# Opening the y accumulation with transposed skip terms made on GpSimd, in place of fp32 products with a diagonal matrix

## The chip, the cores and the metric

The kernel runs on one core of one Trainium2 chip. The metric is the device time of one execution in microseconds (us), the median of several runs. Engines are named PE (TensorE; PEld is its weight load), DVE (VectorE), ACT (ScalarE), POOL (GpSimd) and SP (SyncE, which issues the DMAs here).

## The reference, cut to what matters

Two batches of 1024 tokens with 128 features go through a block with two Mamba scans (forward and backward in time) and then a mixture of experts. What the change touches is the skip term `xc * Dsk`, one scalar of `Dsk` per inner channel (256 channels):

```python
xc = silu(conv(xh))                                   # [B, L, DI], DI = 256
delta = softplus(dt @ dt_w.T + dt_b)
h = h * exp(d_t[:, :, None] * A) + (d_t * u_t)[:, :, None] * B_t[:, None, :]   # 16 states
y = einsum('bds,bs->bd', h, C_t) over all t, + xc * Dsk
y = y * silu(z)
return y @ out_proj.T
```

## The kernel before, in words

The work is cut into four units `u` (two batches by two directions). Within a unit there are 16 states by two halves of 128 channels, so 32 steps; the whole kernel has 128 steps `e`, and step `t` of a unit is `e % 32`. A half has its 128 channels on the partitions and the 1024 tokens along the free dimension.

One step passes through four engines:

- ACT makes the decay `dA` (L565, 128x1024) and scales blocks of `duT` by `B` into `dBuT` (L572, eight 128x256 instructions for each state).
- PE turns (transposes, L1202) the blocks of `dBuT` into PSUM tiles `dBu`, two chunks of 512 tokens. There are three such tiles in turn, so a chunk waits for the scan of the chunk three before it (`scan_done`).
- DVE runs the scan on both chunks (L980 forward, L984 backward) into `hs`, of which there are three buffers. Scan `e` therefore waits until the product `e-3` is done (`hc_done`).
- POOL multiplies `hs` by the row `C` into `hc` (L481, 128x1024). It waits for both scan chunks of the step, for the row's DMA and, from three steps on, for PE to have added the `hc` of three steps before.
- PE adds `hc` to the PSUM accumulator `yT` by eight turns, `y_add(e)` (L1202). PE issues it two steps later, behind the `dBu` chunks of step `e+3` of its order and behind the projection work of that step.

PE's order of a step is written out by hand: both chunks of `dBu(e+1)`, then the step's part of the next unit's projections (items `X`, `Z`, `B`, `BT`, `DT`, `DU`, or the last unit's `YT` and `O`), then `y_start` where `t` is 2 or 3, then `y_add(e-2)`. `turn` at L1202 and `mm` at L1198 are helpers, so nearly all PE instructions have one of these two lines.

`y_start(u, half)` opens the accumulator of a half: it waits until DVE has gated the unit before (`gate_done`, L993), and then multiplies each of eight 128x128 blocks of `xc` with a diagonal matrix `dskip` that holds `D`. An fp32 product is two weight loads and two matmuls in the trace, so one `y_start` is 16 of each.

POOL's order: initial fills, two powers `rstd`, then the loop over all steps. At `t` = 23 and 24 of the first three units it makes `du` of the next unit (L459, 128x1024, two inputs) ahead of that step's product. `du` needs `delta` of the next unit, which ACT makes in two softplus instructions at `t` = 22 (L555) out of the buffer `pre`. The buffer `pre` is then idle until ACT writes it again in the next unit (items `DT`, L540, behind the items `B` and `BT`).

At the start DVE finishes `xc` of unit 0 in two halves (L782, semaphore `x0_ready`) and goes on to scale weights (L823, L825, L830), keep gate rows (L802) and make tap weights (L818).

Of the kernel before, what the change touches and what calls it, by code (L numbers as in the profile page):

```python
# [7 lines left out]
DI, DS, DC, DR = 256, 16, 4, 64  # L8
E, TOPK, F = 8, 64, 512
P = 128  # L10
NH = DI // P
NBLK = L // P
CH = 512
NCH = L // CH
BPC = CH // P
XD = DR + 2 * DS
NU = 2 * NB
# [13 lines left out]
WAT, WCOLS = {}, 0  # L31
# [75 lines left out]
def count_of(it, kinds):  # L107

    return sum(o[0] in kinds for o in ORDER[:NUMBER[it] + 1])


def product_at(e):

    u, t = divmod(e, DS * NH)
    if u + 1 == NU or t not in (SP_AT + 1, SP_AT + 2):
        return None
    return t - SP_AT - 1


def build_block(nc, x_d, mod_d, wpack_d, bcast_d, dtw_d, w1_d, w2_d, crow_d, out_d):  # L120
    fp32 = mybir.dt.float32
    ALU = mybir.AluOpType
# [3 lines left out]
    with ctx:  # L126
        def sb(name, shape):
            return ctx.enter_context(nc.sbuf_tensor(name, shape, fp32))

        def pb(name, shape):  # L130
            return ctx.enter_context(nc.psum_tensor(name, shape, fp32))

        def sem(name):
            return ctx.enter_context(nc.semaphore(name))
# [5 lines left out]
        wp = sb("wp", [P, WCOLS])  # L140
# [8 lines left out]
        xc = [area1[:, p, 0] for p in range(2)]  # L149
# [5 lines left out]
        pre = sb("pre", [P, NH, L])  # L155
# [7 lines left out]
        Cb = area3[:, 3:6, :]  # L163
        yg = area3[:, 6:6 + NH, :]
        du = yg
        wtap = sb("wtap", [P, 2, DC, DI])
        Aneg = sb("Aneg", [P, 2, NH, DS])
        dskip = sb("dskip", [P, 2, NH, P])
# [16 lines left out]
        yT = pb("yT", [P, NH, NBLK, P])  # L185
# [24 lines left out]
        s_w = sem("weights_loaded")  # L210
# [21 lines left out]
        x0_ready = sem("first_x_ready")  # L232
# [9 lines left out]
        tanh_ready = sem("tanh_ready")  # L242
        delta_ready = sem("delta_ready")
        du_ready = sem("du_ready")
        c_stored = sem("c_stored")
        cb_ready = [sem(f"cb_ready{i}") for i in range(3)]
        da_ready = sem("da_ready")
# [54 lines left out]
        def unit(u):  # L302
            return u // 2, u % 2, u % 2

        def wait_item(eng, *it):

            if it[0] in BY_ACT:
                eng.wait_ge(item_act, count_of(it, BY_ACT))
            else:
                eng.wait_ge(item_dve, count_of(it, BY_DVE))  # L310
# [5 lines left out]
        def wait_delta(eng, half, u):  # L316

            if u == 0:
                wait_item(eng, "DT", half * NCH + NCH - 1, 0)
            else:  # L320
                eng.wait_ge(delta_ready, NH * (u - 1) + half + 1)
# [105 lines left out]
        @block.gpsimd  # L427
        def _(g_):
            g_.memset(ident[:, :], 0.0).then_inc(s_c, 1)
            g_.memset(ones[:, :], 1.0).then_inc(s_c, 1)  # L430
            g_.memset(mhalf[:, :], -0.5).then_inc(s_c, 1)
            g_.memset(ones3[:, :], 1.0).then_inc(s_c, 1)
            g_.memset(hT[:, :, :], 0.0).then_inc(s_c, 1)
            g_.memset(emask[:, :, :], 0.0).then_inc(s_c, 1)
            g_.iota(iotak[:, :], [[1, TOPK]], base=1, channel_multiplier=0,
                    allow_small_or_imprecise_dtypes=True).then_inc(s_c, 1)
            g_.wait_ge(s_c, 7)
            g_.affine_select(out=ident[:, :], in_=ident[:, :], compare_op=ALU.not_equal, fill=1.0, base=0,
                             pattern=[[-1, P]], channel_multiplier=1).then_inc(s_c, 1)
            g_.wait_ge(s_c, 8)  # L440

            g_.affine_select(out=emask[0:64, :, :], in_=emask[0:64, :, :], compare_op=ALU.not_equal, fill=1.0,
                             base=0, pattern=[[-2, NPAIR], [1, E]], channel_multiplier=0).then_inc(s_c, 1)
            g_.wait_ge(s_c, 9)
            g_.affine_select(out=emask[64:P, :, :], in_=emask[64:P, :, :], compare_op=ALU.not_equal, fill=1.0,
                             base=-1, pattern=[[-2, NPAIR], [1, E]], channel_multiplier=0).then_inc(s_c, 1)
            g_.wait_ge(s_c, 10)

            for b in range(NB):
                rs = slice(b * NBLK, (b + 1) * NBLK)  # L450
                g_.wait_ge(xvar_ready, b + 1)
                g_.tensor_tensor(rstd[:, rs], rstd[:, rs], mhalf[:, rs], ALU.pow).then_inc(xrstd_ready, 1)

            def pool_du(half, u):
                _, _, par = unit(u)
                wait_delta(g_, half, u)
                for c in range(NCH):
                    wait_item(g_, "X", half * NCH + c, u)
                g_.tensor_tensor(du[:, half, :], delta[par][:, half, :], xc[par][:, half, :],  # L459
                                 ALU.mult).then_inc(du_ready, 1)  # L460

            pows = [0]

            def rstd_pow(b):

                pows[0] += 1
                g_.wait_ge(var_ready, pows[0])
                rs = slice(b * NBLK, (b + 1) * NBLK)
                g_.tensor_tensor(rstd[:, rs], rstd[:, rs], mhalf[:, rs], ALU.pow).then_inc(rstd_ready, 1)

            for e in range(NT):
                g = e // NH
                if product_at(e) is not None:
                    pool_du(product_at(e), e // (DS * NH) + 1)
                if e == NT - 1:
                    break
                g_.wait_ge(scan_done, NCH * (e + 1))
                g_.wait_ge(cb_ready[g % 3], 16 * (g // 3 + 1))
                if e >= 3:
                    g_.wait_ge(yacc_done, e - 2)  # L480
                g_.tensor_tensor(hc[:, e % 3, :], hs[:, e % 3, :], Cb[:, g % 3, :], ALU.mult).then_inc(hc_done, 1)  # L481
                if e - NH * DS * (NU - 2) in POW_AT:
                    rstd_pow(0)
                if e == 0:

                    g_.memset(ones16[:, :], 1.0).then_inc(upto_ready, 1)
                    g_.wait_ge(upto_ready, 1)
                    g_.affine_select(out=upto[:, :], in_=ones16[:, :], compare_op=ALU.is_ge, fill=0.0, base=0,
                                     pattern=[[1, P]], channel_multiplier=-1).then_inc(upto_ready, 1)

            for n in range(2):
                rstd_pow(1)

        @block.scalar
        def _(act):
# [55 lines left out]
            def softplus(u):  # L551
                _, _, par = unit(u)
                wait_item(act, "DT", NH * NCH - 1, u)
                for half in range(NH):
                    nc.scalar.activation(delta[par][:, half, :], pre[:, half, :], ACT.Softplus).then_inc(delta_ready, 1)  # L555

            def exp_tile(e):

                u, s, half = e // (DS * NH), e // NH % DS, e % NH
                _, dr, par = unit(u)  # L560
                if s == 0:
                    wait_delta(act, half, u)
                if e >= 3:
                    act.wait_ge(scan_done, NCH * (e - 2))
                nc.scalar.activation(dA[:, e % 3, :], delta[par][:, half, :], ACT.Exp,  # L565
                                     scale=Aneg[:, dr, half, s:s + 1]).then_inc(da_ready, 1)

            def scale_block(g, n):

                u, s = divmod(g, DS)  # L570
                _, _, par = unit(u)
                return nc.scalar.activation(dBuT[:, g % 2, n, :], duT[par][:, n, :], ACT.Copy,  # L572
                                            scale=bT[:, par, n, s:s + 1])
# [622 lines left out]
        def _(pe):  # L1196
            def mm(out, lhsT, rhs, start, stop):
                return nc.tensor.matmul(out, lhsT, rhs, start=start, stop=stop, skip_group_check=True)  # L1198

            def turn(out, in_, start, idn=None):  # L1200

                return nc.tensor.matmul(out, in_, ident[:, :] if idn is None else idn, start=start, stop=True,  # L1202
                                        is_transpose=True, skip_group_check=True)
# [155 lines left out]
            def y_start(u, half):  # L1359

                _, dr, par = unit(u)
                if u > 0:
                    pe.wait_ge(gate_done, NH * (u - 1) + half + 1)
                for n in range(NBLK):
                    mm(yT[:, half, n, :], xc[par][:, half, n * P:(n + 1) * P], dskip[:, dr, half, :],
                       n % BPC == 0, True)

# [28 lines left out]
            for e in range(NT):  # L1396
                u, t = divmod(e, DS * NH)
# [185 lines left out]
```

## Time and profile before

| | us |
|---|---|
| median of 3 runs | 596.76 (596.41 to 598.2) |
| the profiled execution | 597.98 |
| its span, first to last instruction | 596.2 |
| mean granted TensorE clock | 0.946 |
| PE, DVE, ACT, POOL busy | 497.6, 466.6, 445.2, 330.5 |

A busy time is the sum of an engine's instructions. A row of the timeline gives the start, the duration, engine, line, operation, tiles, shapes and count; the bracket at its end is the idle time of that engine just before, and what ended it. Rows that follow each other on one engine overlap a little, so the time that a group really occupies is read from start to start, or from the chain of waits, which follows the instruction that ended last back to what released it.

### The profile page before, as it was taken

To read this page: it belongs to the slowest core of one execution; us is meant where nothing else is said; L and a number is where in the kernel's file an instruction comes from. 1 tells how busy PE (TensorE), PEld (TensorE's weight loads), DVE (VectorE), ACT (ScalarE), POOL (GpSimd) and SP (SyncE) were. 2 spreads that over 40 slices of the span, in tenths; PEclk is the share of its full clock that TensorE was granted. 3 is DMA by queue.
4 is the path that set the end of the run, shared out by engine and by line. 5 is a ranking of instruction groups with operands and counts; after the bars stand their busy time and mean duration, and the time that the engine had idled before them with its cause. 6 is when DMAs were issued, how large, how long until landed. Compare 5 with 4: busy or idle time off the path is not lost.

```text
span 596.2 us, 9244 instructions
## 1 busy us (share of the span) xinstructions
PE 497.6 (83%) x3378; PEld 409.0 (69%) x3378; DVE 466.6 (78%) x709; ACT 445.2 (75%) x847; POOL 330.5 (55%) x155
## 2 busy tenths in 40 slices
PE   3578979996899999698998896778967486999997
PEld 2245856876788678586965676678856375788696
DVE  5866887976978777699799985988999999866422
ACT  2459865999998789999975899987979761274250
POOL 3104645867966677696766777957667673200000
PEclk9888998998999999799999997979989989978999
DMA  7031120321322222123220231312272214000101
GB/s 256 0 110 37 71 71 36 101 75 38 111 85 90 74 72 71 59 87 106 73 72 35 72 107 36 111 47 95 71 212 76 86 53 142 0 1 2 35 1 36
DMA packets 17885, 43.46 MB, mean 73 GB/s; under 512 B 1328, under 2 KB 7600, under 8 KB 17584
## 3 DMA queue, kind: packets, MB, share of 16 engines
q1 hardware_dynamic: 17840, 42.87, 21.9%
q8 instruction: 27, 0.44, 0.3%
q14 instruction: 18, 0.15, 0.1%
HBM read 41.56 MB, written 1.31 MB: 72 GB/s over the span
## 4 chain that ended last, share of the span: by engine, by line
PE 40%; ACT 28%; DVE 23%; issue 6%; POOL 1%; DMA 1%; POOLq 0%; DVEq 0%; ACTq 0%
ACT dBuT L572 13%; PE pro L1198 11%; DVE area L984 9%; PE yT L1198 9%; PE yT L1202 8%; ACT dA L565 8%; PE dBu L1202 6%; PE dBu L1198 4%; DVE area L980 3%; PE pro L1202 2%; DVE area L772 1%; ACT pre L540 1%; ACT th L533 1%; DVE pre L954 1%; ACT area L555 1%
## 5 line engine op out<-in xcount | busy, mean ns | idle before, releaser
L481 POOL TENSOR_TENSOR hc<-area 128x1024 f32<-128x1024 f32 x127 | 303.2, 2390 | 159.6 <-DVE area L980 92.4
L572 ACT ACTIVATE dBuT<-area,bT 128x256 f32<-128x256 f32 x508 | 215.1, 498 | 13.8 <-PE dBu L1202 13.7
L1202 PE MATMUL dBu<-ident,dBuT 128*128 128x128 f32 x1024 | 147.2, 281 | 43.3 <-DVE area L984 23.5
L565 ACT ACTIVATE dA<-area,Aneg 128x1024 f32<-128x1024 f32 x128 | 146.1, 1142 | 20.3 <-DVE area L984 13.5
L1202 PEld LDWEIGHTS dBu<-ident,dBuT 128*128 128x128 f32 x1024 | 118.1, 144 | 57.3 <-issue 21.3
L1202 PE MATMUL yT<-ident,hc 128*128 128x128 f32 x1024 | 140.3, 282 | 1.7 <-POOL hc L481 1.4
L1202 PEld LDWEIGHTS yT<-ident,hc 128*128 128x128 f32 x1024 | 120.7, 145 | 20.6 <-issue 16.4
L984 DVE TENSOR_TENSOR_SCAN area<-dA,area,dBu 128x512 f32<-128x512 f32 x64 | 81.8, 1278 | 4.5
L980 DVE TENSOR_TENSOR_SCAN area<-dA,area,dBu 128x512 f32<-128x512 f32 x64 | 81.8, 1278 | 4.1
L980 DVE TENSOR_TENSOR_SCAN area<-dA,dBu 128x512 f32<-128x512 f32 x64 | 77.1, 1205 | 7.7 <-PE dBu L1202 7.0
L984 DVE TENSOR_TENSOR_SCAN area<-dA,dBu 128x512 f32<-128x512 f32 x64 | 77.1, 1205 | 6.5 <-PE dBu L1202 6.0
L1198 PE MATMUL pro<-hT,wtap 128*128 128x512 f32 x96 | 48.0, 624 | 0.2 <-DVE area L869 0.2
L1198 PE MATMUL pro<-wp,hT 128*128 128x256 f32 (+1 forms) x96 | 23.2, 372 | 14.3 <-DVE area L869 12.6
L869 DVE SCALAR_TENSOR_TENSOR area<-th,pro 128x512 f32<-128x512 f32 x16 | 11.0, 688 | 25.8 <-ACT th L533 25.3
L533 ACT ACTIVATE th<-pro 128x512 f32<-128x512 f32 x28 | 16.5, 588 | 19.3 <-PE pro L1198 19.3
L1198 PEld LDWEIGHTS pro<-wp,hT 128*128 128x128 f32 x96 | 15.6, 201 | 18.2 <-DVE area L869 14.6
L1202 PE MATMUL pro<-ident,area 128*128 128x128 f32 x108 | 17.4, 285 | 11.2 <-DVE area L869 4.8
L1198 PEld LDWEIGHTS pro<-hT,wtap 128*128 128x128 f32 x96 | 17.3, 201 | 13.3 <-issue 12.6
L1202 PEld LDWEIGHTS pro<-ident,area 128*128 128x128 f32 x108 | 12.2, 143 | 14.2 <-DVE area L869 5.5
L641 ACT ACTIVATE hc<-dBu,modT 128x512 f32<-128x512 f32 x2 | 1.6, 780 | 25.7 <-PE dBu L1198 25.7
L670 ACT ACTIVATE hc<-yT,wp 128x64 f32<-128x64 f32 x64 | 14.0, 330 | 8.5 <-PE yT L1198 8.4
L1198 PE MATMUL pro<-area,wp 128*96 128x512 f32 x28 | 14.7, 643 | 6.3 <-DVE area L782 6.3
(227 smaller groups left out, 570.1 us busy)
## 6 DMA issues: line engine op xcount, KB each, us to landing
area<-c_rows SPq DMA_DIRECT2D x64, 512.0 KB, 3.7
dBuT<-w_in SPq DMA_DIRECT2D x1, 2048.0 KB, 9.2
wp<-wpack_in SPq DMA_DIRECT2D x1, 1030.0 KB, 7.5
x<-x_in SPq DMA_DIRECT2D x2, 512.0 KB, 6.5
hc<-bcast_in SPq DMA_DIRECT2D x1, 1024.0 KB, 10.5
out<-x SPq DMA_DIRECT2D x4, 256.0 KB, 2.4
hT<-w_in SPq DMA_DIRECT2D x1, 512.0 KB, 7.3
acc<-w_in SPq DMA_DIRECT2D x1, 512.0 KB, 7.5
```

The costliest lines, as they stand in the source:

```text
L481: g_.tensor_tensor(hc[:, e % 3, :], hs[:, e % 3, :], Cb[:, g % 3, :], ALU.mult).then_inc(hc_done, 1)
L533: nc.scalar.activation(th[:, :], src, ACT.Tanh).then_inc(tanh_ready, 1)
L540: nc.scalar.activation(dst[:, half, c * CH:(c + 1) * CH], src, func, bias=dtb(dr, half)).then_inc(item_act, 1)
L555: nc.scalar.activation(delta[par][:, half, :], pre[:, half, :], ACT.Softplus).then_inc(delta_ready, 1)
L565: nc.scalar.activation(dA[:, e % 3, :], delta[par][:, half, :], ACT.Exp, scale=Aneg[:, dr, half, s:s + 1]).then_inc(da_ready, 1)
L572: return nc.scalar.activation(dBuT[:, g % 2, n, :], duT[par][:, n, :], ACT.Copy, scale=bT[:, par, n, s:s + 1])
L670: last = nc.scalar.activation(hid[:, q % 2, i, c, :], up_bank(q)[:, at:at + TOPK], ACT.Gelu_apprx_tanh, bias=b1c[:, 2 * q + i, c:c + 1])
L869: nc.vector.scalar_tensor_tensor(gz[par][:, 2 * j:2 * j + 2, :].rearrange("p n d -> p (n d)"), th[:, :], 1.0, src, ALU.add, ALU.mult).then ...
L980: nc.vector.tensor_tensor_scan(hs[:, e % 3, lo:hi], dA[:, e % 3, lo:hi], dBu[q % 3][:, :], init, ALU.mult, ALU.add).then_inc(scan_done, 1)
L984: nc.vector.tensor_tensor_scan(hs[:, e % 3, lo:hi][:, ::-1], dA[:, e % 3, lo:hi][:, ::-1], dBu[q % 3][:, ::-1], init, ALU.mult, ALU.add).t ...
L1198: return nc.tensor.matmul(out, lhsT, rhs, start=start, stop=stop, skip_group_check=True)
L1202: return nc.tensor.matmul(out, in_, ident[:, :] if idn is None else idn, start=start, stop=True, is_transpose=True, skip_group_check=True)
```

## The change: what it does

POOL gets a new instruction, `skip_term(half, u)`: one multiplication of `xc` (128x1024, fp32) by a column of `D`, written to `skip`, which is the buffer `pre` under another name. It is made for units 0, 1 and 2. For unit 0 both halves stand ahead of POOL's loop and wait for `x0_ready`. For units 1 and 2 they stand at `t` = 25 and 26 of the unit before, ahead of that step's product, and wait for `delta_ready` (so that the softplus has read `pre`). In `y_start` of those units PE waits for `skip_ready` and then issues eight turns of `skip` in place of eight fp32 products. The last unit keeps the products, and the diagonal matrices are still built.

```diff
+        skip = pre
+        skip_ready = sem("skip_term_ready")
+            def skip_term(half, u):
+                _, dr, par = unit(u)
+                at = WAT["dskip"] + dr * NH + half
+                if u == 0:
+                    g_.wait_ge(s_w, 16)
+                    g_.wait_ge(x0_ready, half + 1)
+                else:
+                    for c in range(NCH):
+                        wait_item(g_, "X", half * NCH + c, u)
+                    g_.wait_ge(delta_ready, NH * (u - 1) + half + 1)
+                g_.tensor_scalar(skip[:, half, :], xc[par][:, half, :], wp[:, at:at + 1], None,
+                                 ALU.mult).then_inc(skip_ready, 1)
...
+            for half in range(NH):
+                skip_term(half, 0)
             for e in range(NT):
                 g = e // NH
                 if product_at(e) is not None:
                     pool_du(product_at(e), e // (DS * NH) + 1)
+                if product_at(e - 2) is not None and e // (DS * NH) < NU - 2:
+                    skip_term(product_at(e - 2), e // (DS * NH) + 1)
...
             def y_start(u, half):
                 if u > 0:
                     pe.wait_ge(gate_done, NH * (u - 1) + half + 1)
+                if u + 1 < NU:
+                    pe.wait_ge(skip_ready, NH * u + half + 1)
                 for n in range(NBLK):
+                    if u + 1 < NU:
+                        turn(yT[:, half, n, :], skip[:, half, n * P:(n + 1) * P], n % BPC == 0)
+                        continue
                     mm(yT[:, half, n, :], xc[par][:, half, n * P:(n + 1) * P], dskip[:, dr, half, :],
                        n % BPC == 0, True)
```

## Rows read from the trace of the kernel before

**Rows 1.** The chain that ended last, its shares of the span by engine.

```profile
PE 40%; ACT 28%; DVE 23%; issue 6%; POOL 1%; DMA 1%; POOLq 0%; DVEq 0%; ACTq 0%
```

**Rows 2.** The groups of PE's instructions that touch yT: busy us, mean ns, idle before.

```profile
L1202 PE MATMUL yT<-ident,hc 128*128 128x128 f32 x1024 | 140.3, 282 | 1.7 <-POOL hc L481 1.4 <-DVE hc L1118 0.3
L1198 PE MATMUL yT<-dskip,area 128*128 128x128 f32 x128 | 15.7, 276 | 0.0
```

**Rows 3.** The chain of waits, unit 0's opening: start us, us, what.

```profile
57.50 1.78 PE yT L1198 x16
59.28 0.87 PE yT L1202 x8
...
61.89 1.78 PE yT L1198 x16
```

**Rows 4.** Timeline of ACT behind unit 0's opening.

```profile
61.93 0.60 ACT L533 ACTIVATE th<-pro 128x512 f32<-128x512 f32 x1 [0.58 <-PE pro L1198]
...
65.03 1.71 ACT L572 ACTIVATE dBuT<-area,bT 128x256 f32<-128x256 f32 x4 [1.46 <-PE dBu L1202]
```

**Rows 5.** The chain of waits from the end of unit 0 to unit 1's opening.

```profile
160.11 0.66 PE dBu L1202 x4
...
171.61 1.79 PE yT L1198 x16
```

**Rows 6.** Timeline of ACT behind the openings of units 1 and 2.

```profile
178.71 1.71 ACT L572 ACTIVATE dBuT<-area,bT 128x256 f32<-128x256 f32 x4 [1.40 <-PE dBu L1202]
...
289.12 1.31 ACT L572 ACTIVATE dBuT<-area,bT 128x256 f32<-128x256 f32 x3 [1.46 <-PE dBu L1202]
```

**Rows 7.** The groups of POOL's instructions: busy us, mean ns, idle before.

```profile
L481 POOL TENSOR_TENSOR hc<-area 128x1024 f32<-128x1024 f32 x127 | 303.2, 2390 | 159.6 <-DVE area L980 92.4 <-DVE area L984 53.6 <-PE yT L1202 8.8
L433 POOL MEMSET hT<- 128x2060 f32 x1 | 1.8, 1804 | 0.0
L438 POOL TENSOR_SCALAR_AFFINE_SELECT ident<-ident 128x128 f32<-128x128 f32 x1 | 0.3, 292 | 0.2 <-POOL iotak L435 0.2
L445 POOL TENSOR_SCALAR_AFFINE_SELECT emask<-emask 64x32 f32<-64x32 f32 x1 | 0.2, 226 | 0.1
L429 POOL MEMSET ident<- 128x128 f32 x1 | 0.2, 204 | 0.3 <-POOLq L1576 0.3
```

**Rows 8.** The end of unit 0 as one stretch: us, busy of PE, PEld, DVE, ACT, POOL, PEclk, DMA share, GB/s.

```profile
142.00:160.00 18.00, 15.11 (x128) 13.77 (x126) 17.15 (x15) 17.73 (x35) 18.00 (x9) 0.99 0.28 94
```

**Rows 9.** Timelines at unit 0's end: POOL product 26, DVE scans 29 and 32, PE.

```profile
149.54 2.39 POOL L481 TENSOR_TENSOR hc<-area 128x1024 f32<-128x1024 f32 x1
...
152.78 1.19 DVE L980 TENSOR_TENSOR_SCAN area<-dA,dBu 128x512 f32<-128x512 f32 x1
160.27 1.20 DVE L984 TENSOR_TENSOR_SCAN area<-dA,dBu 128x512 f32<-128x512 f32 x1
...
161.47 1.04 PE L1202 MATMUL dBu<-ident,dBuT 128*128 128x128 f32 x8
164.07 0.60 PE L1202 MATMUL yT<-ident,hc 128*128 128x128 f32 x4
```

**Rows 10.** Timelines at unit 1's end: POOL products 57 and 58, DVE scan 61.

```profile
256.21 2.37 POOL L481 TENSOR_TENSOR hc<-area 128x1024 f32<-128x1024 f32 x1 [0.43 <-DVE area L984]
258.70 2.37 POOL L481 TENSOR_TENSOR hc<-area 128x1024 f32<-128x1024 f32 x1
...
263.53 1.20 DVE L984 TENSOR_TENSOR_SCAN area<-dA,dBu 128x512 f32<-128x512 f32 x1
```

**Rows 11.** One group of DVE's L954: count, ns min/median/max, first and last start.

```profile
L954 DVE TENSOR_SCALAR acc<-acc,mv,rstd x8: 323/334/2370, 314.0 to 317.8; 128x128 f32<-128x128 f32 x8
```

**Rows 12.** Timeline of DVE at the start, behind its weight work.

```profile
36.10 0.29 DVE L877 COPY bT<-yT 128x128 f32<-128x128 f32 x1 [1.87 <-PE yT L1202]
38.75 1.23 DVE L787 TENSOR_TENSOR area<-area 128x1024 f32<-128x1024 f32 x1 [2.35 <-ACT area L540]
```

**Rows 13.** The chain of waits behind PE's idle stretch before 139 us.

```profile
140.14 1.71 PE yT L1202 x8
```

## The prediction

> **What bounds the kernel now.** I read the chain of waits first, then the timelines of the engines around the places that the change touches, then the groups. The chain lies on PE for 40% of the span, on ACT for 28 and on DVE for 23 [rows 1], so no busy share decides: each place has to be looked at by itself. Where the accumulators open, the chain runs through PE. In unit 0 the two openings stand on it with 1.78 us each [rows 3], in unit 1 with 1.79 us [rows 5], whose second, at 175.58 us, and the two of unit 2, at 282 and 286 us, repeat the row. Behind each pair ACT sits idle until a dBu tile comes from PE: 0.58 and 1.46 us in unit 0 [rows 4], 1.40 and 1.46 us in units 1 and 2 [rows 6]. These idle times are the most that a faster PE can hand on there. At the end of unit 0 it is different: POOL is busy for 18.00 of 18.00 us, ACT for 17.73 and DVE for 17.15 [rows 8]. POOL's two new instructions of unit 1 fall into just this stretch.
>
> **What PE saves.** An fp32 product is two passes in the trace: 64 products are 128 matmuls [rows 2]. Their own durations (276 against 282 ns) say nothing, since they overlap; the chain gives what a group occupies. Sixteen passes take 1.78 to 1.79 us and eight turns 0.87 us [rows 3, 5]. An opening made of turns thus saves 1.79 - 0.87 = 0.92 us, and a pair 1.84 us. Six openings change, 5.5 us of PE work in all. Unit 3's keep their products.
>
> **What of it counts.** Unit 0: the first opening moves the tanh of ACT earlier by 0.58 us, then ACT is its own limit; at the dBuT group ACT has that 0.58 plus 1.46 us, over 1.84, so all 1.84 us pass through. Unit 1: ACT is busy without a gap until 1.40 us before 178.71 us, so at most 1.40 us pass. Unit 2: at most 1.46 us. Without a cost elsewhere this is 1.84 + 1.40 + 1.46 = 4.70 us. From there on ACT, DVE, POOL and the C rows' DMAs all follow the same steps, and no load from outside is due, so I take the gain as kept.
>
> **What one multiplication costs on POOL.** The trace shows no such instruction at this size. From below: a fill takes (1804 - 204) / (2060 - 128) = 0.83 ns per column, so 1024 columns take 204 + 896 x 0.83 = 0.95 us; the affine selects, which read and write, give (292 - 226) / (128 - 32) = 0.69 ns per column and 0.91 us [rows 7]. From above: the same size with two inputs takes 2.36 to 2.39 us [rows 7]. The new instruction reads one tile and writes one, as the select does, so I take X = 1.0 us and keep 0.9 and 2.36.
>
> A page leaves room for more. The Trainium skill, GPSIMD Engine Reference, section "Performance versus the Vector engine", has 1.03 cycles per element at 1.2 GHz for the lightest loop bodies and about 1.8 for a tight loop with more in it, estimates of 0.88 and 1.54 us here; by the dearer one the sum below would be 3.3 us of gain instead of 4.4. The short rows of this trace stand near the first, but no run shows the size in question.
>
> **Where it delays, unit 0's end.** The first multiplication stands ahead of product 25, the second ahead of product 26, and POOL has no gap to take them. Product 26 ended at 149.54 + 2.39 = 151.93 us, scan 29, which waits for its buffer, began at 152.78 [rows 9]. The slack is 0.85 us, so with X = 1.0 scan 29 is 2.0 - 0.85 = 1.15 us late. Behind it DVE runs back to back and doesn't catch up. What waits for DVE is PE: the second chunk of dBu(33), at 161.47 + 4 x 0.11 = 161.91 us, needs the tile that the first chunk of scan 32 frees at 160.27 + 1.20 = 161.47 us; a slack of about 0.4. PE comes 1.15 - 0.4 = 0.75 us late, and it is on the chain from there to unit 1's openings [rows 5]. y_add(30), at 164.07 us, is not hit: product 30, four products further, ended at about 151.93 + 4 x 2.36 = 161.4, a slack of 2.7 us, more than 2X. Queued behind the two multiplications are POOL's products alone; it issues no DMA. PE's pair of openings then has 1.84 - 0.75 = 1.09 us to give, under the cap of 1.40. Unit 1's share falls from 1.40 to 1.09 us.
>
> **Unit 1's end.** Product 58 ended at 261.07 us, scan 61 began at 263.53: 2.46 us of slack, and POOL has a gap of 0.43 us ahead of product 57 [rows 10]. With PE's 0.4 us of slack behind DVE this covers 2X up to 3.3 us: no cost up to X = 1.6 us.
>
> **The start.** Unit 0's multiplications come as soon as the halves of `xc` are finished, around 29 to 31 us; POOL's loop has nothing to do until the first scan. DVE then has its TENSOR_SCALAR instructions (L823 to L830). One such instruction, 334 ns in the median, took 2370 ns once, beside a product of POOL [rows 11]; so they may be held for as long as POOL works, some 1 to 2 us. DVE then waits 1.87 us for PE and 2.35 us for ACT [rows 12], which covers it; without this cover the start would be 1 to 2 us longer. The B products need only `xc`, which is finished before. The new wait of PE for `skip_ready` is met some 20 us or more before each opening.
>
> **The sum.** 1.84 + 1.09 + 1.46 = 4.4 us. The profiled execution's own time is 597.98 us, its span of 596.2 and 1.8 around it; it would be 593.6. It is 1.2 us above the median of 596.76, from which the same gain gives 592.4 us, the forecast.
>
> **The rivals.** A first one is that the multiplication costs what a two-input product does, X = 2.36 us. Scan 29 is then 4.72 - 0.85 = 3.87 us late and PE 3.47, so unit 1's share is 1.84 - 3.47 = -1.63 us. At unit 1's end PE is 4.72 - 0.43 - 2.46 - 0.4 = 1.43 us late, so unit 2's share is 0.41. The sum is 0.6 us of gain, 596.1 us. For it speaks that POOL has no other full-size row; against it the slopes of rows 7.
>
> The second ends on the other side: the multiplication with a column operand runs far below the rate of the shorter rows, at twice a product's time, 4.7 us. Along the same steps the sum is 1.84 + (3.09 - 2X) + (5.13 - 2X) = 10.1 - 4X, so the change costs time from X = 2.5 us, and 4.7 us would cost 8.7 us, 605.5 us. For it speaks only that no row shows a column operand on POOL; every row of the group lies far below.
>
> The third is that the clock does not hold under turns. At the lower of its two levels eight turns take 1.71 us [rows 13]. Openings of turns would then save 0.08 us each, and the sum is 0.16 + (0.16 - 0.75) + 0.16 = -0.3, 597.0 us; each further group of eight turns at that level would add 0.84. Against it: in the stretch from 142 to 160 us PE did nothing but turns, and the granted clock was 0.99, so the full 2.4 GHz [rows 8]. The Trainium skill, TensorE: Matmul & The Clock Gate, section "PE-mode transpose", says that the full clock does not engage for transpose mode; by that rule the turns would be at 1.2 GHz, and the trace disagrees.
>
> The fourth is that only part arrives: the gain is used up later where other engines were equally late (DVE's gates, the first norm), leaving 1 to 2 us, 595.3 us. The chain's steady passing between PE and ACT speaks for it a little; that all engines shift together speaks against.
>
> **How the numbers follow.** I give my forecast 0.72, the two-input price 0.08, the dear multiplication 0.04, the clock 0.03 and the partial gain 0.13. The forecast's own range runs from X = 0.9 with no loss, 4.7 us, to 3 us of gain, and 1 us either way for the clock's steps: 591.0 to 594.8. The range takes in the two-input and the partial case, 591.0 to 596.2 us. A difference under 0.3% (1.8 us) can't be told from none here. Faster by more than that is the forecast and half of the partial case, 0.78; the rest of that case and the two-input price make 0.15 within it; slower 0.07.
>
> **What would show it.** Right, if the chain shows the openings of units 0 to 2 as eight turns of 0.87 us; if POOL's new group has six instructions of about 1.0 us; if scan 29 comes about 1.2 us later against scan 26 than now, and PE's idle time there grows; if ACT's idle time behind units 1 and 2's openings nearly vanishes. Wrong, if the new group's mean lies above 1.6 us, if PE or DVE wait for POOL at the end of unit 1 too, if the granted clock falls in the openings, or if unit 0's first opening, at 57.5 us, moves.

## The result: 599.71 us against 597.3 us, a little slower

The changed kernel has a median of 599.71 us in 14 runs, the kernel before 597.3 us in 14 runs beside it. The ratio of the changed kernel to the one before is 1.0036, with a 95% interval of 1.002 to 1.0052. The profiled execution took 599.41 us, its span is 597.7 us, the mean granted clock 0.94 (before: 0.946). In the experiments below, four executions fell in a slower state (600.29 and 728.93 us with the later multiplications, 950.73 us with turns only, 605.32 us with unit 0 alone): the medians count them, the ratios don't.

The chain of the changed kernel by engine, and who waits for POOL's products (us in total, times, longest):

```profile
PE 41%; DVE 25%; ACT 20%; issue 8%; POOL 3%; DMA 1%; POOLq 0%; DVEq 0%; ACTq 0%
```

```profile
PE yT L1222 <- POOL hc L501: 7.3, 6, 2.0
...
DVE area L1000 <- POOL hc L501: 4.7, 2, 2.5
DVE area L1004 <- POOL hc L501: 2.4, 1, 2.4
```

Against [rows 1] ACT has lost 8 points of the chain, and POOL and idle "issue" time have come in. DVE's waits for POOL's products are new, and PE's had been 1.4 us. The line numbers are 20 higher than before from L481 on.

**The price.** The new instruction on POOL: count, ns min/median/max, first and last start.

```profile
L475 POOL TENSOR_SCALAR pre<-area,wp x6: 2837/2883/4826, 29.0 to 261.6; 128x1024 f32<-128x1024 f32 x6
```

The forecast put 1.0 us on it. It takes 2.8 to 2.9 us in the loop, more than the two-input product of [rows 7], and the two at the start take 8.81 us together beside DVE's work.

**Where time came and went.** Starts of the same scans and groups in the two profiled executions, after less before, in us:

| place | difference | what changed it |
|---|---|---|
| PE's first turns of hc, behind unit 0's first opening | -0.2 | start 0.7 later, first opening 0.9 shorter |
| scan 6 | -1.1 | second opening |
| scan 12 | -2.1 | a low-clock stretch at 88 us is 3.4 us long in place of 6.8 |
| scan 29 | +2.8 | POOL's two multiplications at the end of unit 0 (4.9 us since scan 24, at -2.1) |
| scan 38 | +0.65 | unit 1's openings give back what they can |
| scan 61 | +3.3 | the end of unit 1 |
| scan 64 | +3.8 | the end of unit 1, with PE behind it |
| scan 70 | +1.9 | unit 2's openings |
| end of the span | +1.5 | clock steps at 362 us and behind |

The end of unit 0, POOL and then DVE of the changed kernel:

```profile
145.14 2.88 POOL L475 TENSOR_SCALAR pre<-area,wp 128x1024 f32<-128x1024 f32 x1
147.95 2.39 POOL L501 TENSOR_TENSOR hc<-area 128x1024 f32<-128x1024 f32 x1
150.27 2.88 POOL L475 TENSOR_SCALAR pre<-area,wp 128x1024 f32<-128x1024 f32 x1
153.09 16.33 POOL L501 TENSOR_TENSOR hc<-area 128x1024 f32<-128x1024 f32 x7
```

```profile
150.42 1.22 DVE L1000 TENSOR_TENSOR_SCAN area<-dA,dBu 128x512 f32<-128x512 f32 x1 [2.12 <-POOL hc L501]
...
155.57 1.22 DVE L1000 TENSOR_TENSOR_SCAN area<-dA,dBu 128x512 f32<-128x512 f32 x1 [2.54 <-POOL hc L501]
```

Product 26 starts at 153.09 us in place of 149.54 [rows 9], and scan 29 waits 2.54 us for it. PE comes to the second chunk of dBu(33) and on to unit 1's openings later; the chain comes there from POOL's products and DVE's scans now, where it came from ACT before. In this stretch PE stands idle for POOL (2.02 and 1.68 us), and the granted clock falls:

```profile
142.00:160.00 18.00, 13.42 (x99) 11.77 (x97) 12.79 (x11) 15.18 (x28) 18.00 (x8) 0.91 0.22 72
```

It was 0.99 there [rows 8]; PE's turns of 150.39 us then take 1.75 us a group of eight where others take 1.09. PE's idle wait comes first, the lower level (1.2 GHz) after it.

At the end of unit 1 it goes the same way. PE waits for the product behind the second multiplication, its turns stand at the lower level, and the clock of the stretch is 0.91 where the kernel before has 1.00:

```profile
266.80 1.97 PE L1222 MATMUL yT<-ident,hc 128*128 128x128 f32 x8 [1.69 <-POOL hc L501]
```

```profile
256.00:275.00 19.00, 15.91 (x122) 14.47 (x121) 15.65 (x14) 18.02 (x36) 19.00 (x9) 0.91 0.19 62
```

```profile
256.00:275.00 19.00, 16.77 (x130) 14.10 (x129) 17.98 (x16) 19.00 (x38) 17.95 (x8) 1.00 0.29 91
```

The first of these two stretches is the changed kernel's, the second that of the kernel before. The traces of the experiments repeat it. Where PE's longest wait for POOL at an end was 1.50 to 3.17 us, the clock of that stretch was 0.90 or 0.91: at both ends with POOL's side alone, at unit 0's end with the cheaper form, at unit 1's end with only that end loaded. At all the other ends it was 0.99 to 1.00; PE did not wait for POOL there, or 0.20 us with the cheaper form and at most 1.33 us with the copy. What these low stretches cost by themselves was not separated.

PE's side did what was foretold. The chain through the openings of units 0 and 1:

```profile
58.22 1.75 PE yT L1222 x16
...
174.08 1.75 PE yT L1222 x16
```

These rows merge the opening's eight turns and the eight of hc behind them: 1.75 us, where the opening alone took 1.78 to 1.79 [rows 3, 5] and the hc turns 0.87 more. That is 0.9 us an opening, as worked out. Behind them ACT's idle time is 0.33, 0.49 and 0.49 us in place of 1.46, 1.40 and 1.46 [rows 4, 6].

### The profile page after: what moved, and what is told of

Its sections match the earlier page's. It is cut to its first block, busy times and chain, and to the rows that moved or that the text cites. A ratio compares the mean times of both kernels' runs of the same rounds, so it can differ in the third digit from the quotient of the medians.

```text
span 597.7 us, 9164 instructions
## 1 busy us (share of the span) xinstructions
PE 497.0 (83%) x3330; PEld 407.3 (68%) x3330; DVE 467.0 (78%) x709; ACT 445.7 (75%) x847; POOL 350.5 (59%) x161
## 4 chain that ended last, share of the span: by engine, by line
PE 41%; DVE 25%; ACT 20%; issue 8%; POOL 3%; DMA 1%; POOLq 0%; DVEq 0%; ACTq 0%
PE pro L1218 11%; PE yT L1222 10%; DVE area L1004 10%; ACT dBuT L592 9%; PE yT L1218 7%; PE dBu L1222 7%; DVE area L1000 5%; ACT dA L585 5%; PE dBu L1218 4%; POOL hc L501 2%; PE pro L1222 2%; DVE area L792 1%; ACT pre L560 1%; DVE pre L974 1%; ACT area L575 1%
## 5 line engine op out<-in xcount | busy, mean ns | idle before, releaser
L1222 PE MATMUL dBu<-ident,dBuT 128*128 128x128 f32 x1024 | 149.3, 285 | 40.6 <-DVE area L1004 23.9
L1222 PEld LDWEIGHTS dBu<-ident,dBuT 128*128 128x128 f32 x1024 | 121.0, 146 | 53.7 <-issue 21.8
L1222 PE MATMUL yT<-ident,hc 128*128 128x128 f32 x1024 | 142.2, 285 | 7.6 <-POOL hc L501 7.3
L475 POOL TENSOR_SCALAR pre<-area,wp 128x1024 f32<-128x1024 f32 x6 | 20.3, 3379 | 12.0 <-DVE area L802 12.0
```

What stands on the lines that cost most here:

```text
L475: g_.tensor_scalar(skip[:, half, :], xc[par][:, half, :], wp[:, at:at + 1], None, ALU.mult).then_inc(skip_ready, 1)
```

## The experiments

Theory A, where no other is stated, is that PE's gain is real and that the price and place of POOL's multiplication spend it.

### PE's side alone

```diff
-                        turn(yT[:, half, n, :], skip[:, half, n * P:(n + 1) * P], n % BPC == 0)
+                        turn(yT[:, half, n, :], xc[par][:, half, n * P:(n + 1) * P], n % BPC == 0)
```

with no multiplication and no wait for it (`D` is left out of `y` in units 0 to 2).

> No multiplication on POOL: PE turns xc itself in units 0 to 2, so D is left out of y there. Theory A: PE's side alone, the caps of ACT's idle time give 1.84 + 1.40 + 1.46 = 4.7 us of gain, 592.6 us. Theory B (the clock doesn't hold under turns in place of products): 0 to 1 us of gain at most, with a granted clock under that of before.

Measured: 593.84 us, before 597.49; ratio 0.9934 (0.9912 to 0.9956), 3.7 us of gain by the medians. Unit 0's opening in the chain, and the end of unit 0:

```profile
56.89 1.75 PE yT L1218 x16
```

```profile
142.00:160.00 18.00, 15.84 (x131) 14.09 (x130) 16.66 (x14) 18.00 (x35) 17.90 (x8) 1.00 0.27 93
```

The turns gain, and the granted clock is 1.00 in a stretch made of them. Theory B falls for this stretch. The mean clock of the profiled execution was 0.939, under that of before: scan 80 starts 6.25 us before that of the kernel before, scan 84 only 4.67, and between them, at 332 us, lies a low-clock stretch of 3.4 us that the kernel before doesn't have. It takes back 1.6 us. Step by step the trace gives what was expected: unit 0's openings gain 1.8 us (scan 0 to 6), unit 1's 1.3 (scan 24 to 40) and unit 2's 1.6 (scan 60 to 72), 4.7 in all. What brings the stretch at 332 us about was not tried.

### POOL's side alone

```diff
                 for n in range(NBLK):
-                    if u + 1 < NU:
-                        turn(yT[:, half, n, :], skip[:, half, n * P:(n + 1) * P], n % BPC == 0)
-                        continue
```

> POOL multiplies as in the change and PE waits for it, but keeps its fp32 products. Theory A: the cost side alone. Two times 2.82 us less 1.25 us of slack is 4.4 us at the end of unit 0, two times 2.82 less 3.3 is 2.3 us at the end of unit 1, together 6.7 us longer, about 604 us. Theory B: the multiplications are hidden, at most 2 us longer.

Measured: 604.69 us, ratio 1.0112 (1.0094 to 1.013), 7.2 us longer. Expected were 6.7 from slack and price. Its chain at the end of unit 0:

```profile
163.76 0.66 PE dBu L1222 x4
```

This is the second chunk of dBu(33), which stood at about 161.91 us before, now 1.85 us later, although scan 24 had been 2.7 us earlier by a clock step: 4.6 us lost at this end for 4.4 expected. The end of unit 1 costs 2.7 us (scan 56 is 1.90 us late, scan 72 4.62) for 2.3 expected. The 0.4 us of slack that PE has behind DVE at unit 0's end does not show at unit 1's: the lateness is 4.62 us at scan 64 and still 4.62 at scan 72, while behind unit 0's end it falls from 2.25 at scan 32 to 1.91 at scan 34. Without that term the price and slack give 2 x 2.82 - 0.43 - 2.46 = 2.75 us there.

The two sides add up to 7.2 - 3.7 = 3.5 us, and the change itself costs 2.4. They are not simply additive: in the prediction's sum 0.44 and 0.38 us of PE's gain, which ACT could not use in units 1 and 2, go against the lateness. The rest of the difference is smaller than the runs can tell.

### The same multiplications where POOL has gaps

```diff
-                if product_at(e - 2) is not None and e // (DS * NH) < NU - 2:
-                    skip_term(product_at(e - 2), e // (DS * NH) + 1)
+                if 0 < e // (DS * NH) < NU - 1 and e % (DS * NH) in (1, 2):
+                    skip_term(e % (DS * NH) - 1, e // (DS * NH))
```

> The multiplications of units 1 and 2 stand at t = 1 and 2 of the unit itself, ahead of products 33, 34, 65 and 66, in place of t = 25 and 26 of the unit before. Theory A (place and price: a multiplication holds POOL for 2.8 us, and at the ends of units 0 and 1 there is no slack for it): at t = 1 and 2 POOL has gaps of 1.7 and 2.2 us and the products 4.8 us or more until PE adds them, so nothing is late and PE's gain of 4.7 us is kept: about 592.6 us. Theory B (turns or the multiplications bring the granted clock down wherever they stand): no faster than before, 597 us or more, at a clock of 0.943 or less.

Measured: 594.08 us, ratio 0.9935 (0.9921 to 0.9948). It is the same as with no multiplication at all (0.9934), at the full price:

```profile
163.36 2.84 POOL L475 TENSOR_SCALAR pre<-area,wp 128x1024 f32<-128x1024 f32 x1
166.16 2.37 POOL L501 TENSOR_TENSOR hc<-area 128x1024 f32<-128x1024 f32 x1
168.52 2.84 POOL L475 TENSOR_SCALAR pre<-area,wp 128x1024 f32<-128x1024 f32 x1
```

No engine waits for POOL more than before, and the clock at the ends of units 0 and 1 is 0.99 and 1.00. The place decides. The mean clock was 0.939 here too, with the gain, so a lower mean clock does not explain the change's loss by itself. Theory A had put 592.6 us: the trace has the same low-clock stretch at 333 us as the one with turns only, where 1.6 us go, and the one execution with a mean clock of 0.951 took 591.39 us.

### Unit 0 alone

```diff
-                if u + 1 < NU:
+                if u == 0:
```

in `y_start`, and no multiplication in the loop.

> Multiplications and turns for unit 0 alone. Theory A: the multiplications at 29 to 38 us are hidden behind DVE's and PE's other work, and unit 0's openings give 1.84 us: 595.4 us. Rival C (the start pays: DVE's TENSOR_SCALAR work is held beside POOL, or PE's clock falls there): the first scan is 1 us later, and the gain is under 1 us, 596.5 us or more.

Measured: 595.66 us, before 597.49, ratio 0.9963 (0.9948 to 0.9978): 1.8 us by the medians and 2.2 by the ratio, for 1.84 in Theory A. In the trace scan 6 starts 1.82 us earlier and scan 0 at the same time. The start, DVE, first the kernel before and then this one:

```profile
30.26 0.19 DVE L825 TENSOR_SCALAR Aneg<-Aneg 128x64 f32<-128x64 f32 x1
```

```profile
30.16 1.03 DVE L843 TENSOR_SCALAR Aneg<-Aneg 128x64 f32<-128x64 f32 x1
...
46.49 1.22 DVE L998 TENSOR_TENSOR_SCAN area<-dA,dBu 128x512 f32<-128x512 f32 x1 [1.34 <-PE dBu L1220]
```

DVE is held, 1.03 us for an instruction of 64 columns that took 0.19, but the first scan starts at 46.49 us, the same time as before. The cover held. So the 1.2 us by which the first scan of the changed kernel's profile is late is not the multiplications'. It went with another position and length of the low-clock stretches at the start: the second of them is 6.8 us long from 44.8 us in place of 3.4 us from 46.9. The copy's trace below has the same stretches and the same 1.2 us.

### What POOL charges for what

The kernel before with 30 instructions behind POOL's last one:

```diff
+            for _ in range(2):
+                for n in (1024, 512, 128):
+                    probe(g_.tensor_scalar(dst[:, 0:n], src[:, 0:n], col, None, ALU.mult))
+                    probe(g_.tensor_scalar(dst[:, 0:n], src[:, 0:n], 1.5, None, ALU.mult))
+                    probe(g_.tensor_copy(dst[:, 0:n], src[:, 0:n]))
+                    probe(g_.tensor_tensor(dst[:, 0:n], src[:, 0:n], src2[:, 0:n], ALU.mult))
+                    probe(g_.tensor_tensor(dst[:, 0:n], src[:, 0:n], col.to_broadcast([P, n]), ALU.mult))
```

> The kernel before, with 30 extra POOL instructions behind its last one, where POOL is idle: 128 rows by 1024, 512 and 128 columns, each as multiplication by a column, by an immediate number, copy, product of two tiles, and product with a column broadcast along the row, all twice. They write a tile that nothing reads. Theory E (the column operand makes it dear): by a column 2.8 us at 1024, by an immediate about 1.0, copy about 1.0, two tiles 2.36. Theory F (POOL's TENSOR_SCALAR as a whole is slow): column and immediate both 2.8 us, 2.7 ns per further column of the tile, only the copy about 1.0.

The timeline of POOL: the five forms at 1024 columns in the order of the code (second round), then the multiplication by a column at 512 and at 128 columns (first round):

```profile
541.71 2.84 POOL L506 TENSOR_SCALAR area<-area,wp 128x1024 f32<-128x1024 f32 x1
544.64 2.77 POOL L507 TENSOR_SCALAR area<-area 128x1024 f32<-128x1024 f32 x1
547.48 1.04 POOL L508 COPY area<-area 128x1024 f32<-128x1024 f32 x1
548.60 2.35 POOL L509 TENSOR_TENSOR area<-area 128x1024 f32<-128x1024 f32 x1
551.03 1.89 POOL L510 TENSOR_TENSOR area<-area,wp 128x1024 f32<-128x1024 f32 x1
...
532.65 1.56 POOL L506 TENSOR_SCALAR area<-area,wp 128x512 f32<-128x512 f32 x1
...
539.03 0.60 POOL L506 TENSOR_SCALAR area<-area,wp 128x128 f32<-128x128 f32 x1
```

Theory E falls: the immediate costs 2.77 us, so the column adds 0.07. Theory F stands, with (2.84 - 1.56) / 512 = 2.5 ns per column. The copy, at 1.04 us, is what the forecast had priced. And the same multiplication written as a product with a broadcast column costs 1.89 us, a third less, and less than a product of two tiles. The execution took 608.15 us in its one run. With POOL busy at the tail, DVE's work there is held (last section), which is part of it; the rest was not looked into.

### The cheaper form at the old place

```diff
-                g_.tensor_scalar(skip[:, half, :], xc[par][:, half, :], wp[:, at:at + 1], None,
-                                 ALU.mult).then_inc(skip_ready, 1)
+                g_.tensor_tensor(skip[:, half, :], xc[par][:, half, :], wp[:, at:at + 1].to_broadcast([P, L]),
+                                 ALU.mult).then_inc(skip_ready, 1)
```

> As the change, but the six multiplications are TENSOR_TENSOR with D's column broadcast along the row. Theory A (the price decides, the sum is 10.1 - 4X): at the price of a two-tile product, 2.36 us in place of 2.82, the four multiplications in the loop come 1.8 us cheaper, about 597.9 us where the change takes 599.7. If the broadcast costs as much as the column, 599.7 us.

Measured: 594.49 us, before 597.62, ratio 0.9947 (0.9929 to 0.9965). The expectation took the wrong price, 2.36 us:

```profile
L475 POOL TENSOR_TENSOR pre<-area,wp x6: 1897/1903/2823, 29.0 to 258.5; 128x1024 f32<-128x1024 f32 x6
```

With X = 1.90 the prediction's own sum, 10.1 - 4X, gives 2.5 us of gain; 3.1 came by the medians. The clock fell at the end of unit 0 here too (0.91), behind a wait of PE of 2.20 us, and not at the end of unit 1 (1.00). One instruction exchanged for another turns the change from slower to faster.

### The price of the forecast

```diff
-                g_.tensor_scalar(skip[:, half, :], xc[par][:, half, :], wp[:, at:at + 1], None,
-                                 ALU.mult).then_inc(skip_ready, 1)
+                g_.tensor_copy(skip[:, half, :], xc[par][:, half, :]).then_inc(skip_ready, 1)
```

> As the change, but POOL copies xc into the idle buffer in place of multiplying it (D is left out of y in units 0 to 2). A copy of this size took 1.04 us on POOL alone, which is the price that the prediction had put on the multiplication. Theory A (the steps of the prediction hold and only the price was wrong): 1.84 + (3.09 - 2.08) + 1.46 = 4.3 us of gain, about 593.3 us. Rival G (a new wait and a filled POOL queue cost more than the price says): 595.5 us or more.

Measured: 593.73 us, before 597.52, ratio 0.9937 (0.9923 to 0.9951), 3.8 us of gain. POOL's copy and the scan that waits:

```profile
L475 POOL COPY pre<-area x6: 1031/1045/1970, 29.0 to 256.0; 128x1024 f32<-128x1024 f32 x6
```

```profile
151.90 1.22 DVE L999 TENSOR_TENSOR_SCAN area<-dA,dBu 128x512 f32<-128x512 f32 x1 [0.70 <-POOL hc L500]
```

At the forecast's price the forecast's steps come out one by one: scan 24 is 2.06 us earlier than in the kernel before, scan 29 only 0.88, so it lost 1.18 us (worked out: 1.15). From scan 24 to scan 40 unit 1 gained 0.95 us net (1.09), and from scan 60 to scan 72 unit 2 gained 1.60 (1.46). Rival G falls.

### One end spared

```diff
-                if product_at(e - 2) is not None and e // (DS * NH) < NU - 2:
+                if product_at(e - 2) is not None and e // (DS * NH) == 1:
                     skip_term(product_at(e - 2), e // (DS * NH) + 1)
+                if e // (DS * NH) == 1 and e % (DS * NH) in (1, 2):
+                    skip_term(e % (DS * NH) - 1, 1)
```

> Unit 1's multiplications at its own t = 1 and 2, unit 2's at the end of unit 1 as in the change. Theory A (slack less price, end by end): the end of unit 0 costs nothing, the end of unit 1 costs 2 x 2.82 - 3.3 = 2.3 us; 1.84 + 1.40 + (1.84 - 2.3) = 2.8 us of gain, about 594.7 us. Rival D (POOL's lateness is paid in full wherever the multiplication stands early, 5.6 us an end): 1.84 + 1.40 + 1.84 - 5.6 = -0.5, 598 us.

Measured: 594.3 us, before 597.62, ratio 0.9942 (0.9922 to 0.9962), 3.3 us of gain where Theory A says 2.8 and rival D -0.5. Rival D falls: lateness is price less slack, end by end. In its trace the end of unit 1 costs scan 64 2.9 us against scan 60 (-3.99 to -1.08, after less before), and unit 2's openings give 1.8 back by scan 72. Of the 0.6 us by which the 2.9 exceed the expected 2.3, PE's missing slack is 0.4; the clock of this end was low too (0.91).

### All four units

As above with the multiplications at t = 1 and 2, and unit 3 too, into the idle `delta` buffer:

```diff
+                dst = skip if u + 1 < NU else delta[1 - par]
...
-                for dr in range(2):
-                    for half in range(NH):
-                        at = WAT["dskip"] + dr * NH + half
-                        last = nc.vector.tensor_scalar(dskip[:, dr, half, :], ident[:, :], wp[:, at:at + 1], None, ALU.mult)
```

So two things differ from that kernel: unit 3's openings, and DVE's diagonal matrices at the start, which are no longer built.

> As the kernel with the multiplications at t = 1 and 2, and unit 3 does the same (its products go into the delta buffer of the other parity, which unit 3 doesn't use); the diagonal matrices are not built any more. Theory A: unit 3's openings give up to another 1.8 us over that kernel, 592.3 to 593.3 us. Rival: unit 3 is bound elsewhere (DVE's extra work of the expert selection) and nothing more comes, 594.1 us.

Measured: 597.26 us, before 597.62, ratio 0.9997 (0.9967 to 1.0027), in 12 runs of 593.8 to 602.6 us. The runs fall into groups by their mean granted clock: five with 0.945 lie at 593.8 to 594.9, two with 0.934 at 596.9 and 597.6, five with 0.926 at 600.1 to 602.6. Unit 3's opening of the profiled execution, in the chain:

```profile
399.02 3.19 PE yT L1219 x16
```

It is at the lower level for the most part (1.75 us elsewhere). Whether the changed openings bring the low clock about, and how, stays open; one execution of the kernel with three changed units also had 0.926 and took 600.29 us. The five runs at 0.945 lie where the rival put them, the others lie higher than either expectation, and no gain is shown.

### Both cures

The broadcast form at t = 1 and 2, units 1 and 2 (and unit 0 at the start): the diffs of the cheaper form and of the multiplications where POOL has gaps, together.

> Both cures at once: the multiplication as a product with the broadcast column (1.89 us) and, in units 1 and 2, at t = 1 and 2 of the unit itself. Theory A: place and price cure the same lateness, so no more comes than from the place alone: 593.5 to 594.2 us. Rival: POOL's lighter load shows at t = 1 and 2 too, 593 us or less.

Measured: 592.09 us, before 597.52, ratio 0.992 (0.99 to 0.9939), 5.4 us of gain by the medians, the lowest median of all.

```profile
162.98 1.90 POOL L475 TENSOR_TENSOR pre<-area,wp 128x1024 f32<-128x1024 f32 x1
164.83 2.37 POOL L501 TENSOR_TENSOR hc<-area 128x1024 f32<-128x1024 f32 x1
167.16 1.90 POOL L475 TENSOR_TENSOR pre<-area,wp 128x1024 f32<-128x1024 f32 x1
```

```profile
142.00:160.00 18.00, 15.37 (x123) 13.40 (x123) 17.27 (x16) 18.00 (x35) 18.00 (x9) 1.00 0.30 101
```

Its interval overlaps that of the same place with the dearer form (0.9921 to 0.9948), so the rival is not shown, and the runs speak for Theory A. No engine waits for POOL more in either. Three runs had a mean clock of 0.951 and lie at 591.0 to 591.4 us, three had 0.939 and lie at 592.8 to 594.0; the kernel with the dearer form took 591.39 us in its one run at 0.951 and 593.0 to 594.2 in its seven at 0.939. At the same clock the two agree, and the lower median here comes of three runs in six at the higher clock against one in ten. This trace has no low-clock stretch at 333 us, where that one loses 1.6 us. Why the clock takes one course or the other stays open.

This trace also shows the openings with little clock in the way: unit 0's give 1.8 us (scan 0 to 6), unit 1's 1.8 (scan 24 to 40) and unit 2's 1.6 (scan 60 to 72).

## Why the prediction was wrong, step by step

- **What PE saves: right.** Eight turns for sixteen passes give 0.9 us an opening on the chain, in units 0, 1 and 2 (the merged rows of 1.75 us).
- **What of it counts: right.** ACT's idle time behind the openings was about the cap: 1.8, 1.3 and 1.6 us came in the trace without multiplications for 1.84, 1.40 and 1.46, and 1.8, 1.8 and 1.6 with both cures, so the caps of units 1 and 2 were not strict: that trace has 0.4 and 0.1 us more. That the medians show 3.7 us for 4.70 goes with the clock, above all with a low-clock stretch at 332 us that the kernel before doesn't have; the prediction took the gain as kept.
- **What one multiplication costs: this is the step that failed.** I took X = 1.0 us, from the slopes of a fill and an affine select, because the new instruction reads and writes one tile "as the select does". It is 2.82 us from start to start, and lies outside the bounds of 0.9 and 2.36 that I kept. A two-input product is no upper bound for a one-input multiplication on this engine: the rows of another operation bounded nothing. With a copy in its place, which takes the 1.04 us of the forecast (and leaves `D` out), the change is 3.8 us faster than the kernel before.
- **Where it delays: right at unit 0's end, 0.4 us off at unit 1's.** The slack of 0.85 us ahead of scan 29 and PE's 0.4 us behind it held: with the copy the scan was 1.18 us late for 1.15. At unit 1's end I carried PE's 0.4 us over without a row for it, and it is not there: that end costs 2.7 us with POOL's side alone, for 2.3. Together POOL's side alone cost 7.2 us for 6.7.
- **The start: right.** DVE was held for about 0.8 us and the cover took it.
- **The rivals.** The second one, with 0.04, comes nearest: its sum, 10.1 - 4X, costs time from X = 2.5 us. Its reason and its price were wrong, though. The column operand adds only 0.07 us, the operation as a whole is dear, and it takes 2.84 us and not 4.7. With X = 2.82 the sum is -1.2 us; -2.4 were measured by the medians. The changed kernel's trace has -2.7 us from scan 24 to scan 40, where the sum gives 3.09 - 2X = -2.55, and -1.3 from scan 56 to scan 72, where 5.13 - 2X gives -0.5; the 0.4 us that PE lacks at unit 1's end are part of this, and the low clock there may be. The difference also goes with the mean clock of a run: the five runs of the changed kernel at 0.946 and 0.948 have a median of 597.6 us, like the kernel before, and the nine at 0.943 and 0.940 one of 600.3. The 1 us either way that the prediction allowed for the clock was too little.
- **The turns and the clock.** The third rival, turns that don't hold the clock, falls: the stretch of turns alone, 142 to 160 us, has 0.99 to 1.00 in eight of the eleven kernels, and 0.90 or 0.91 in the three where PE had just stood idle for POOL. The trace disagrees here with the sentence of the Trainium skill that I weighed (TensorE: Matmul & The Clock Gate, section "PE-mode transpose").
- The 1.8 cycles per element of the Trainium skill's GPSIMD Engine Reference (section "Performance versus the Vector engine"), an estimate of 1.54 us, was nearer than my value, and still too low against 2.84 us; the copy, 1.04 us, stands nearer to its 1.03 cycles, an estimate of 0.88 us.

## What to carry to other kernels

Price an instruction by its own opcode on its own engine: on POOL here the same multiplication costs 2.84 us as TENSOR_SCALAR and 1.89 us as TENSOR_TENSOR with a broadcast column, and if no row shows the form, the range has to reach well past the dearest neighbour. Work added to an engine off the chain costs its length less the slack at that very place; move it to where the engine has gaps (here 18 us later) and the same instructions cost nothing that these runs can tell. Read the slack at each place anew: 0.4 us that were there at one end were missing at the next. Behind a wait that idles PE a low-clock stretch may come on top.

## What the runs showed of the hardware

- POOL's rates at 128 x 1024 fp32, alone: copy 1.04 us, product with a broadcast column 1.89, product of two tiles 2.35, TENSOR_SCALAR 2.77 by an immediate and 2.84 by a column.
- POOL and DVE hold each other up. In the probe, whose extra work runs at the tail, DVE's eight one-hot compares take 4.89 us while POOL is idle and 7.59 us beside it (the same eight take 4.91 us in the kernel before), and POOL's 128-column TENSOR_SCALAR takes 1.44 us for 0.60:

```profile
502.19 4.89 DVE L1055 TENSOR_TENSOR area<-th,iotak 128x512 f32<-128x512 f32 x8
...
556.94 7.59 DVE L1055 TENSOR_TENSOR area<-th,iotak 128x512 f32<-128x512 f32 x8
```

```profile
559.73 1.44 POOL L506 TENSOR_SCALAR area<-area,wp 128x128 f32<-128x128 f32 x1
```

- On PE eight 128x128 fp32 turns occupy 0.87 us at the full clock and 1.71 us at the lower level [rows 13], sixteen passes of eight fp32 products 1.79 us at the full clock.
- In four kernels PE stood idle for POOL at an end of a unit, with a longest wait of 1.50 to 3.17 us. Each time a stretch of 3.4 us at the lower level began, within 1.1 us of that wait's end.
- Runs of one kernel on one core differ by several us with the mean granted clock: the changed kernel's 14 runs lie at 596.5 to 598.7 us with 0.946 or 0.948, and at 599.4 to 602.4 us with 0.943 or 0.940. It is no simple scale: the kernel before took 598.8 to 599.0 us at 0.949 and 596.0 to 598.2 at 0.945 and 0.946.
